# Maxima rows transposed in f32 and split by VectorE, maxima nine steps ahead, LayerNorm items cut in two

## The reference, cut to what matters

```
# block 0 (adaptive LayerNorm from 2 context vectors); x0, x1 are the halves of x (1024 tokens each)
x0 = x0 + g * MHA(mod(ln(x0)));  x1 = x1 + g * MHA(mod(ln(x1)))        # each half attends to itself
x0, x1: q of one half attends to k, v of the other half, gated, added  # crossing attention
x = x + g * gelu(mod(ln(x)) @ fc1) @ fc2
# block 1
x = LN(x + MHA(x, x, x, mask));  x = LN(x + MHA(x, ctx, ctx));  x = LN(x + relu(x @ w1) @ w2)
# everywhere: softmax(q k^T / 4) v, with the row maximum subtracted before the exponential
```

## Time and profile before

| what | value |
|---|---|
| median of 3 runs | 2199.81 us (2197.55 to 2200.25) |
| time of the profiled execution | 2213.78 us |
| its span | 2211.9 us |
| mean granted TensorE clock | 0.945 |
| TensorE (matmul) busy | 1987.0 us, 90% |
| VectorE busy | 1542.5 us, 70% |
| ScalarE busy | 1292.8 us, 58% |
| GpSimd busy | 565.4 us, 26% |

### The profile page before, as it was taken

How to read it: one execution, slowest core, us unless ns; L and a number is a source line. 1 busy time by engine, 2 the same in 40 slices (tenths; PEclk the granted TensorE clock), 3 DMA queues, 4 the chain that set the end, 5 groups by cost and what they waited for, 6 DMA issues and landing times. The chain is left out here.

```text
span 2211.9 us, 33881 instructions
## 1 busy us (share of the span) xinstructions
PE 1987.0 (90%) x12890; PEld 774.5 (35%) x12890; DVE 1542.5 (70%) x2841; ACT 1292.8 (58%) x2406; POOL 565.4 (26%) x537
## 2 busy tenths in 40 slices
PE   5798888899999899898999899899999999999976
PEld 3333222332233252443433433223335235234315
DVE  4567678788867739456557477788995895896714
ACT  1045566566745577665767655456874774784570
POOL 1025675663032300113121244212020011101100
PEclk8589999999999999999999999879999999999998
DMA  6724333240134302016213254220020020000000
GB/s 154 136 67 103 92 99 100 78 107 25 40 95 90 92 3 48 10 39 142 35 31 68 51 143 90 62 52 25 7 47 3 16 43 4 13 16 4 13 16 12
DMA packets 96251, 125.62 MB, mean 57 GB/s; under 512 B 25262, under 2 KB 80927, under 8 KB 90959
## 3 DMA queue, kind: packets, MB, share of 16 engines
q1 hardware_dynamic: 93774, 122.84, 23.8%
q10 hardware_dynamic: 2304, 0.53, 0.1%
HBM read 88.90 MB, written 24.74 MB: 51 GB/s over the span
## 5 line engine op out<-in xcount | busy, mean ns | idle before, releaser
L1693 ACT ACTIVATE PT<-ps 128x512 f32<-128x512 f32 (+1 forms) x2112 | 1109.3, 602 | 700.2 <-PE ps L1478 697.2
L1776 DVE TENSOR_REDUCE mx<-ps 128x1 f32<-128x512 f32 x2048 | 1284.4, 683 | 270.1 <-PE ps L1499 267.4
L1478 PE MATMUL ps<-QS,KS 51*128 51x512 bf16 (+3 forms) x4224 | 817.5, 388 | 39.1 <-DMA QS<-mr 38.7
L1499 PE MATMUL ps<-KS,QS 49*128 49x512 bf16 x2048 | 735.5, 395 | 99.8 <-DVE mx L1776 57.0
L1525 PE MATMUL ps<-PT,Vt 128*32 128x512 f32 (+1 forms) x4224 | 579.7, 621 | 0.0
L1499 PEld LDWEIGHTS ps<-KS,QS 49*128 49x128 bf16 x2048 | 187.9, 95 | 713.4 <-DVE mx L1776 450.3
L1478 PEld LDWEIGHTS ps<-QS,KS 51*128 51x128 bf16 (+3 forms) x4224 | 237.5, 96 | 261.3 <-ACT PT L1693 51.2
L2010 POOL CAST nm<-nm 128x16 bf16<-128x16 f32 x64 | 12.7, 198 | 540.9 <-DVE nm L1789 540.9
L1525 PEld LDWEIGHTS ps<-PT,Vt 128*32 128x32 f32 (+1 forms) x4224 | 84.0, 109 | 146.5 <-issue 144.2
L1620 PE MATMUL ps<-XT,big 128*128 128x256 f32 x512 | 124.1, 392 | 3.4 <-ACT big L1749 2.7
L1632 PE MATMUL ps<-big 128*128 128x256 f32 x512 | 114.8, 382 | 1.6 <-DVE big L1911 1.6
(11 more groups left out here) (110 smaller groups left out, 1097.4 us busy)
## 6 DMA issues: line engine op xcount, KB each, us to landing
scr<-S SPq DMA_DIRECT2D x27, 768.0 KB, 3.8
big<-in_mask_1x1xSxS_ik SPq DMA_DIRECT2D x16, 1024.0 KB, 5.1
QS<-scr SPq DMA_DIRECT2D x32, 384.0 KB, 10.2
KS<-scr SPq DMA_DIRECT2D x24, 384.0 KB, 8.9
QS<-scr SPq DMA_DIRECT2D x32, 256.0 KB, 7.1
ON<-Oe SPq DMA_DIRECT2D x256, 32.0 KB, 1.9
OD<-scr_r SPq DMA_DIRECT2D x32, 256.0 KB
KS<-scr SPq DMA_DIRECT2D x24, 256.0 KB, 4.9
```

Of the source, the lines that this page charges most:

```text
L1478: z = eng.matmul(ps[0:w, it.bank[1 - j], :], KS[lo:hi, part, pr, col:col + w], QS[lo:hi, part, u.qs, pr, :], start=part == 0, stop=part == ...
L1499: return eng.matmul(mbank(it)[:, 0:w], QS[lo:lo + MR, 0, u.qs, pr, 128 * it.tq:128 * it.tq + 128], KS[lo:lo + MR, 0, pr, it.lo:it.hi], sta ...
L1693: eng.activation(PT[0:w, it.pt * 4 + 2 * it.pp + 1 - k, :], ps[0:w, it.bank[k], :], ACT.Exp, scale=0.25).then_inc(S["exp_done"], 1)
L1776: eng.tensor_reduce(out=mx[:, u.b, c, it.i:it.i + 1], in_=mbank(it)[:, 0:it.hi - it.lo], axis=AX.X, op=ALU.max).then_inc(S["max_done"], 1)
```

## The change

Four things change.

1. The maxima are complete nine steps ahead of their unit instead of seven.
2. GpSimd no longer splits `nm`. TensorE transposes the f32 `nm` itself (128 by 16), and VectorE makes both parts from the transposed result in PSUM: a copy to bf16 and a subtraction, with a semaphore between them.
3. `stats` (four `bn_stats`, four `bn_aggr`) becomes two items one step apart: `bn` with the first two `bn_stats`, then `stats` with the other two and the four `bn_aggr`. This holds for every LayerNorm but the first two and those of the last chunk's tail.
4. `xnorm` (four `tensor_scalar`) becomes two items of two, one step apart, for all but the first two.

In the diff the first `fin_b` is TensorE's part, the second VectorE's, and the last hunk, `fin_a`, is GpSimd's.

```diff
-LEAD = 7
+LEAD = 9
...
-        mr = sb("mr", [32, 2, P], BF16)
+        mr = sb("mr", [16, 2, 2, P], BF16)
...
+        def stats_steps(c, eps, b, wait):
+            return [(wait, lambda: do_bn(c, b, 0, 2)), (1, lambda: do_stats(c, eps, b, 0, 4, 2))]
+
+        def xnorm_steps(c, wait):
+            return [(wait, lambda: do_xnorm(c, 0, 2)), (1, lambda: do_xnorm(c, 2, 2))]
...
         def ln_l1(c, gl, b):
-            return [(DL[3], lambda: do_stats(c, 1e-5, b)), (DL[4], lambda: do_lnscale(c, gl, b))]
+            return stats_steps(c, 1e-5, b, DL[3]) + [(DL[4], lambda: do_lnscale(c, gl, b))]
...
         def ln_mod(c, g):
-            return [(4, lambda: do_stats(c, 1e-6)), (7 if g == 0 else 3, lambda: do_xnorm(c)), (3, lambda: do_xt("mod", c, g))]
+            return (stats_steps(c, 1e-6, 0, 4) + xnorm_steps(c, 7 if g == 0 else 3)
+                    + [(3, lambda: do_xt("mod", c, g))])
...
                 elif it.kind == "fin_b":
-                    q.wait_ge(S["nm_split"], it.split)
-                    eng.transpose(mbank(it)[0:32, 0:64].bitcast(BF16), nm2[:, it.u.b, :, :].rearrange("p t k -> p (t k)"),
-                                  identB[:]).then_inc(S["m_ready"], 1)
+                    q.wait_ge(S["nm_ready"], it.nm)
+                    q.wait_ge(S["ident"], 2)
+                    eng.transpose(mbank(it)[0:16, 0:P], nm[:, it.u.b, :], identF[:]).then_inc(S["m_ready"], 1)
...
                 elif it.kind == "fin_b":
                     q.wait_ge(S["m_ready"], it.m_ready)
                     q.wait_ge(S["m_in"], it.mr_free)
-                    eng.tensor_copy(mr[:, it.u.b, :], mbank(it)[0:32, 0:64].bitcast(BF16)).then_inc(S["mr_done"], 1)
+                    o = mbank(it)[0:16, 0:P]
+                    eng.tensor_copy(mr[:, it.u.b, 0, :], o).then_inc(S["mr_hi"], 1)
+                    q.wait_ge(S["mr_hi"], it.hi)
+                    eng.tensor_tensor(mr[:, it.u.b, 1, :], o, mr[:, it.u.b, 0, :], ALU.subtract).then_inc(S["mr_done"], 1)
...
-                if it.kind == "fin_a":
-                    b = it.u.b
-                    q.wait_ge(S["nm_ready"], it.nm)
-                    q.wait_ge(S["m_ready"], it.nm2_free)
-                    eng.tensor_copy(nm2[:, b, 0, :], nm[:, b, :]).then_inc(S["nm_split"], 1)
-                    q.wait_ge(S["nm_split"], it.split - 1)
-                    eng.tensor_tensor(nm2[:, b, 1, :], nm[:, b, :], nm2[:, b, 0, :], ALU.subtract).then_inc(S["nm_split"], 1)
```

More of the change, by code:

```diff
@@ L77, in xattn_kernel @@
         sems("max_done", "exp_done", "o_free")
-        sems("nm_ready", "nm_split", "mr_done", "m_in")
+        sems("nm_ready", "mr_hi", "mr_done", "m_in")
         sems("st_done", "mv_done", "rs_add", "rs_done", "ln_applied", "xt_act", "xt_dve")
@@ L132, in xattn_kernel @@
         nm = sb("nm", [P, 2, 16], F32)
-        nm2 = sb("nm2", [P, 2, 2, 16], BF16)
-        mr = sb("mr", [32, 2, P], BF16)
+        mr = sb("mr", [16, 2, 2, P], BF16)
         dd = sb("dd", [P, 2, 64], F32)
@@ L211, in x_state, with do_stats @@
             it.x_in, it.x_done = n[f"x_in{c}"], n[f"x_done{c}"]
-        def do_stats(c, eps, b=0, lo=0, nt=4):
+        def do_stats(c, eps, b=0, lo=0, nt=4, bn=None):
             it = item("stats")
-            it.b, it.lo, it.nt = b, lo, nt
+            it.b, it.lo, it.nt, it.bn = b, lo, nt, lo if bn is None else bn
             it.c, it.eps = c, eps
@@ L220, in do_stats, with do_bn, do_xnorm @@
             it.add, it.rs = up("rs_add"), up("rs_done")
-        def do_xnorm(c):
+        def do_bn(c, b, lo, nt):
+            it = item("bn")
+            it.c, it.b, it.lo, it.nt = c, b, lo, nt
+            x_state(it, c)
+            up("st_done")
+        def stats_steps(c, eps, b, wait):
+            return [(wait, lambda: do_bn(c, b, 0, 2)), (1, lambda: do_stats(c, eps, b, 0, 4, 2))]
+        def xnorm_steps(c, wait):
+            return [(wait, lambda: do_xnorm(c, 0, 2)), (1, lambda: do_xnorm(c, 2, 2))]
+        def do_xnorm(c, lo=0, nt=4):
             flush_ends()
             it = item("xnorm")
+            it.lo, it.nt = lo, nt
             it.c, it.rs, it.xn_free = c, n["rs_done"], mark["xn_free"]
@@ L409, in fin_a @@
                 mark["mx_free", u.b] = it.nm
[L410 to L413, removed]
                 fins.append([0, fin_b])
@@ L417, in fin_b @@
                 it = item("fin_b")
-                it.u, it.split, it.last = u, u.split, u.last.m_ready
+                it.u, it.nm, it.last = u, u.nm, u.last.m_ready
                 take_m(it)
-                mark["nm2_free", u.b] = it.m_ready
+                mark["nm_free", u.b] = it.m_ready
                 it.mr_free = mark.get(("mr_free", u.b), 0)
+                it.hi = up("mr_hi")
                 it.mr = up("mr_done")
@@ L1702, in act_part @@
                     for t in range(2):
-                        load(eng, QS[49 + t:50 + t + 64:64, 0, u.qs, 2 * u.hg:2 * u.hg + 2, :], mr[16 * t:16 * t + 16, u.b, :],
+                        load(eng, QS[49 + t:50 + t + 64:64, 0, u.qs, 2 * u.hg:2 * u.hg + 2, :], mr[:, u.b, t, :],
                              "m_in")
@@ L1787, in dve_part @@
                     q.wait_ge(S["max_done"], it.red)
-                    q.wait_ge(S["nm_split"], it.nm_free)
+                    q.wait_ge(S["m_ready"], it.nm_free)
                     eng.tensor_reduce(out=nm[:, u.b, :], in_=mx[:, u.b, :, 0:u.nparts], axis=AX.X, op=ALU.max,
@@ L1797, in dve_part @@
                     q.wait_ge(S[f"x_done{it.c}"], it.x_done)
-                    for t in range(it.lo, it.lo + it.nt):
+                    for t in range(it.bn, it.lo + it.nt):
                         z = eng.bn_stats(st[:, it.b, t, :], x[:, 4 * it.c + t, :])
@@ L1805, in dve_part @@
                     z.then_inc(S["mv_done"], 1)
+                elif it.kind == "bn":
+                    q.wait_ge(S[f"x_in{it.c}"], it.x_in)
+                    q.wait_ge(S[f"x_done{it.c}"], it.x_done)
+                    for t in range(it.lo, it.lo + it.nt):
+                        z = eng.bn_stats(st[:, it.b, t, :], x[:, 4 * it.c + t, :])
+                    z.then_inc(S["st_done"], 1)
                 elif it.kind == "xnorm":
@@ L1808, in dve_part @@
                     q.wait_ge(S[it.xn_free[0]], it.xn_free[1])
-                    for t in range(4):
+                    for t in range(it.lo, it.lo + it.nt):
                         z = eng.tensor_scalar(xn[:, t, :], x[:, 4 * it.c + t, :], mv[:, 0, t, 0:1], rs[:, 0, t:t + 1],
@@ L2005, in pool_part @@
             for it in items:
[L2006 to L2013 removed]
+                if it.kind == "stats":
                     q.wait_ge(S["mv_done"], it.mv)
```

## The result

The changed kernel takes 2164.57 us, the median of four executions (2159.53 to 2170.91); the kernel before took 2198.68 us beside it (2193.55 to 2200.25). The ratio is 0.985, 95% interval 0.9819 to 0.9882: 33 us less. The forecast was 2149.3 us, with 2122 to 2188 as its range.

What follows compares the result with a forecast made beforehand. TensorE, 90% busy, was taken to lose time in waits and the low clock behind them, tied to a nearly full VectorE in attention. Gains of 66 us less 15.5 lost, net 50.5, gave 2149.3 us, range 2122 to 2188.

Steps and rivals of the forecast that it cites:

- the three meetings: TensorE's transposition waiting for GpSimd, busy with a LayerNorm's affine part, once in each of three chunks; one wait is 2.79 us.
- the 27.5 and 12 of the forecast: Net gains: nine steps of lead, 36 us less 8.5 of costs; statistics and normalisation in halves, 12 us.
- six waits in units behind the first: Scores waiting for rows of maxima, 29.3 us in all; the longer lead was to save 25, bounds 10 and 29.
- the first unit's 9.4 us: Longest wait for the rows of maxima, in the very first unit; said to stay, since nothing runs ahead there.
- Unit 16's rows: Maxima of unit 16 waiting for their chunk's query rows: 4.5 us more with its clock, bounds 3 and 8.
- the 5 us that stood for the first: Cost of VectorE's added subtraction, mostly fitting into idle holes; bounds nothing and 22 us.
- The rival in which VectorE sets the end: VectorE's 22 us paid in full, the bursts give nothing: net 21 us, 2178 us; chance 0.12.
- A burst of 0.7 us is then absorbed: Half a group of statistics on VectorE costs TensorE no wait; with the second half's 0.4 us more, 0.1 left.
- The lower bound, nothing: Halves gain nothing where VectorE is nearly full: a pause only spreads the same work, and later maxima come as late.
- New meetings: Transfers of maxima moving relative to key rows of the first units: 3 us lost, bounds 0 and 10.
- queue's gain missing: Rival: maxima transfers stay behind query rows, so the lead gives 10 + 4 instead of 36; 2171 us, chance 0.2.
- many new meetings: Slower rival: maxima fall behind query and key rows in more units; 2220 us with 14 such cases, chance 0.07.

Runs made afterwards that it cites:

- experiment 2: Kernel before with only the lead of the maxima raised from seven to nine steps: 2172.02 us, 0.9876.
- experiment 4: Kernel before with only the statistics and normalisation each cut into two items: 2182.95 us, 0.9943.
- 11: Kernel before with only the statistics cut into two items: 2183.07 us, 0.992.
- experiment 10: Changed kernel with eleven steps of lead, and the reload of the softmax reciprocals served before queued key rows are released: 2155.53 us, 0.9811.
- experiment 1: Changed kernel with the lead back at seven steps: 2184.49 us, 0.9928.
- experiment 3: Kernel before with only the split of `nm` moved to VectorE, behind an f32 transposition: 2185.91 us, 0.9939.
- 6: Kernel before with nine steps of lead and VectorE's split, statistics and normalisation whole: 2171.37 us, 0.9887.
- experiment 12: Kernel before with only the normalisation cut into two items: 2195.81 us, 0.999.
- experiment 8: Changed kernel with VectorE's subtraction done twice, once into a buffer nothing reads: 2165.07 us, 0.986.
- experiment 9: Changed kernel with the reload of the softmax reciprocals served before queued key rows are released: 2162.65 us, 0.9838.
- 5: Changed kernel with the statistics whole again, normalisation still in halves: 2175.99 us, 0.9905.
- experiment 7: Changed kernel with halves kept but chains as long as before, each first half one step earlier: 2174.24 us, 0.9902.

## Why the forecast was right in kind and 15 us too low

**Two terms were too big, and luck hid it in the experiments.** Net, 50.5 us were forecast and 33 measured. The prediction saw the three meetings and gave them to part 2 alone, so its sum has them once, which is right. It did not ask whether part 1 or part 3, which move work by one or two steps, would take them away too. They did, in experiments 2, 4 and 11. These meetings are a matter of a step or two, and each of the shifts ended them as well as the repair. That is why 27 us in experiment 2 and 12.5 in experiment 4 look like the 27.5 and 12 of the forecast: 11 us of each are the meetings, which the forecast had not put there. Without them part 1 is worth 16 instead of 27.5, since its waits shrank by less than forecast, and the halves 1.5 instead of 12, since VectorE did not absorb them. These two misses, with 2 us more than forecast for part 2, give 31.

**Part 1: the mechanism right, the size too big.** An earlier issue gains its two steps and often the place ahead of the query rows, as the timelines of experiment 10 show. The worth, apart from the meetings, is 17 us (experiment 1 against the changed kernel), 16 (27 - 11 from 2) or 11 (3 against 6). Predicted, with its costs, were 36 - 8.5 = 27.5. Two terms were off. Of the six waits in units behind the first, 29.3 us, there are 11.2 left: 18.1 gained, not 25, since two meetings with query rows remained. In the pairs that differ in the lead alone it is less still: 15.9 us from before to 2, 10.1 from 1 to the changed kernel, 11.1 from 3 to 6. And the first unit's 9.4 us did not stay, as it was said to: it is 1.5 us in the changed kernel. Most of that is hardly the change's doing. In the profile of before, the query rows were issued at 82.91 us and the maxima behind them at 84.09. In experiment 3, with the same lead and the same LayerNorm, `nm` was ready 2.7 us sooner than before, the maxima went at 81.34 and the query rows at 82.35, and the wait was 3.81 us. In experiment 12 the maxima went at 78.59, and it was 3.12 us. In experiment 1 they went at 83.95, behind the rows at 83.23, and it was 7.98 us. So this one is a meeting in the queue too, and its order changes with how the start of the kernel runs in one execution: experiment 8 is the changed kernel up to its first subtraction, and has `nm` ready at 82.48 us where that had it at 78.15. The mean clock up to the first score is 0.77 to 0.79 in before, 1 and 8, and 0.82 to 0.85 in 3, 12 and the changed kernel. What sets that isn't shown.

**Unit 16's rows.** Predicted to grow from 6.00 to about 9 us, they grew to 7.18 at nine steps, and to 10.82 at eleven. The direction was right and the size of nine steps too big.

**Part 2: right alone, nothing behind part 1.** 13 us were measured and 11 predicted. The transposition and the copy cost 3.3 + 4.3 us where the sum had 2; the 4 of the copy stood in a sentence beside it. A second subtraction cost nothing that experiment 8 could find; it can't tell 0 from the 5 us that stood for the first. The copy and the subtraction take 0.55 us, as forecast. The rival in which VectorE sets the end is out. So part 2 is worth its 13 us only where nothing else has moved the meetings.

**Parts 3 and 4: the right number by the wrong reason.** "A burst of 0.7 us is then absorbed" failed. A half leaves 0.21 us and the next 0.92, because VectorE hasn't caught up between them; L1509's waits for VectorE are 57.3 us, not the 40 that were to show it. The lower bound, nothing, was the right value for the bursts as far as these waits show, and the argument for it was in the prediction. The 12.5 us measured come mostly from the shifted meetings.

**New meetings.** 3 us were put down for them, for transfers of maxima alone. One came elsewhere, 8.10 us at L1618, and in experiment 9 its removal saved no measurable time, since another wait took its place. TensorE's waits for GpSimd at the transposition of LayerNorm's output grew as well, from 3.5 to 6.6 us. The rivals with the queue's gain missing or with many new meetings are out: QS<-mr fell to 12.7 us. That this is near the 14 forecast is luck: behind the first unit some 4 us were to be left, and 11.2 are; the first unit, which was to keep its 9.4, made up for it.

**The span.** The 2125 to 2168 us that the prediction gives for its own terms have no working; its terms at their bounds add up to some 2110 to 2222 us. The measured time lies in both, so neither was tested.

**What stays open.** The changed kernel is 7 to 11 us shorter than experiments 5, 6 and 7, by their medians, and all kernels with chains two steps longer and nine steps of lead (the changed one, 8, 9) stand at 0.984 to 0.986 against 0.989 to 0.991. Their mean clock is 0.958 to 0.961 against 0.952 to 0.956. The traces show where that lies: in crossing attention and self-attention, from the 513th to the 1281st exponential.

```
                      length    TensorE idle    at the lower clock level
changed kernel        865.0 us      67.1              58.0
8  double subtraction 869.2            68.4              58.0
9  reload first       866.2            63.8              68.3
5  stats whole        874.9            67.6              81.9
6  no halves          876.6            66.1              88.7
7  halves, as before  872.9            61.5              85.3
```

TensorE idles as long in both groups. The second three are 8.0 us longer on the mean, and spend 23.9 us more at the lower level; at 0.32 that is 7.7 us. So by these records the difference is clock. One place of it can be named, here in experiment 7:

```profile
990.83 0.55 DVE L1880 RECIPROCAL dd<-dd 128x64 f32<-128x64 f32 x1 [3.97 <-DMA dd<-Oe]
...
992.08 0.60 PE L1509 MATMUL ps<-KS,QS 49*128 49x512 bf16 x1 [4.15 <-DVE mx L1786]
```

```profile
990.90:997.70 6.80, 5.62 (x23) 2.15 (x23) 4.13 (x8) 0.77 (x2) 0.00 (x0) 0.50 0.38 103
```

VectorE comes to the reciprocal ahead of its operand, TensorE runs out of maxima, and the clock is at the lower level for 6.8 us (the second fence is a window, columns as in the earlier trace rows). Before, 2, 3, 5, 6, 7, 11 and 12 all have this wait, 3.8 to 5.5 us long; the kernels with chains two steps longer (the changed one, 1, 4, 8, 9, 10) do not, and VectorE waits for nothing there. So the longer chains ended this meeting. In exchange 1, 4, 8 and the changed kernel have the 8 to 9 us at L1618, and 9 and 10 have 6.0 and 6.8 us for query rows. Why the balance in the clock comes out in their favour with nine steps, and not with seven (4 takes 885.3 us for this stretch, before 883.5), the runs don't tell; nor do they show what the halves do apart from the length of the chain, beyond 7 being no faster than 6.

## What to carry to other kernels

Before adding up what several edits gain, write beside each wait which of the edits would remove it, also by merely moving work a step; a wait counts once. Test it by running each part alone and all together: if the product and the whole differ, look for a stretch whose length takes only two values over all variants. A part that alone gives what was forecast may do so by another mechanism; look in its trace for the waits that were to go. A wait that a repair removes from the trace has paid only if no later wait on the same engine grows by as much.

## What the runs showed of the hardware

The price of a low clock could be read a second way. Over the four executions of the changed kernel the time goes from 2159.53 us at a mean granted clock of 0.963 to 2170.91 at 0.955, 14 us for 0.01. 0.01 of the mean is 43 us at the lower level (0.50), so by these four a third of such a window is lost, near the 0.32 of the output matmuls. It is a rough price: the executions of the other kernels give 8 to 27 us for 0.01. One and the same program thus spreads by 11 us, a third of the whole gain, with the clock.

Transfers issued by ScalarE landed late when SyncE's six had been issued ahead of them, 14.6 us from issue to the score at 358 us, and in time when issued ahead. The first unit gives both cases, since its score waits for these transfers in each of five profiles. Issued 0.7 to 1.2 us behind the six (before, 1), the score came 10.1 and 8.6 us after the issue; issued 1.0 to 4.4 us ahead of them (3, 12, the changed kernel), 3.4 to 4.4 us after it. The Trainium skill (DMA: Bandwidth & Descriptors, section "Queues, rings and completion order") has the engines take the queues' packets in turn; the difference by order speaks against an even share, but no run here has these two queues alone.
